# Graph network in four layers: TensorE adds half of the attention heads while turning them, elu in four VectorE operations, convolution tables packed side by side

## What is computed

```python
edge_index = jnp.stack([src, dst])
x = _layernorm(x + _L0_gnn_ref(x, edge_index, edge_weight, ...))   # two TAG convolutions of 5 hops
x = _layernorm(x + _L1_gnn_ref(x, edge_index, ...))                # mean aggregation, then attention with 4 heads
x = _layernorm(x + _L2_gnn_ref(x, edge_index, edge_weight1, ...))  # sum/mean convolution
x = _layernorm(x + _L3_gnn_ref(x, edge_index, ...))                # attention with 4 heads, dense layer
```

```python
def _tag_conv(x, row, col, norm, W, b):        # layer 0, called twice
    out = x @ W[0]
    h = x
    for k in range(1, K + 1):                  # K = 5
        h = jax.ops.segment_sum(h[row] * norm[:, None], col, num_segments=N_NODES)
        out = out + h @ W[k]
    return out + b
# end of layer 1: out is the mean of the heads
out = (out - mu) * jax.lax.rsqrt(var + 1e-05) * gamma + beta
return jax.nn.elu(out)
```

## Time and profile before

| | |
|---|---|
| median of three runs | 10347.91 us (10343.13 to 10349.23) |
| the profiled execution's own time | 10350.19 us |
| its span in the trace | 10348.5 us |
| PE, PEld, DVE busy | 56%, 28%, 57% of the span |
| ACT, POOL busy | 31%, 67% |
| granted TensorE clock, mean | 0.768 |
| DMA | 1016.84 MB, mean 98 GB/s |

### The profile page before, as it was taken

One profiled execution on the slowest core, in us unless ns is written; L12 is line 12 of the kernel. 1 busy time (PEld: TensorE's weight loads), 2 busy tenths in 40 slices (PEclk: granted clock), 3 DMA queues, 4 the chain that ended last, 5 costly groups with the idle time before them and its releaser, 6 DMA issues. The chain is left out here.

```text
span 10348.5 us, 86417 instructions
## 1 busy us (share of the span) xinstructions
PE 5760.6 (56%) x19261; PEld 2887.3 (28%) x19261; DVE 5897.1 (57%) x16861; ACT 3169.7 (31%) x5395; POOL 6886.8 (67%) x6659
## 2 busy tenths in 40 slices
PE   1672465555566984555555400598885776720277
PEld 0331232333333542222222200243222333410143
DVE  2341565556555656666666578544449994520697
ACT  0351233333332322222222201244443553310144
POOL 7777777777777747777777777775750006767477
PEclk9796677777777996676666655799998997755698
DMA  4620332222224752222222222222333442222353
GB/s 130 202 84 20 84 109 89 89 86 92 87 90 156 245 206 83 89 88 85 86 89 86 82 74 80 69 72 57 72 61 111 146 139 63 75 52 52 81 151 121
DMA packets 967572, 1016.84 MB, mean 98 GB/s; under 512 B 530229, under 2 KB 584231, under 8 KB 954507
## 3 DMA queue, kind: packets, MB, share of 16 engines
q1 hardware_dynamic: 754186, 880.78, 26.3%
q0 software_dynamic: 212864, 130.53, 7.1%
HBM read 491.86 MB, written 596.27 MB: 105 GB/s over the span
## 5 line engine op out<-in xcount | busy, mean ns | idle before, releaser
L710 POOL DMA_INDIRECT gathered<-u,place_of_source x1564 | 1645.0, 1052 | 522.5 <-issue 476.3
L710 POOL DMA_INDIRECT gathered<-hop,place_of_source x1564 | 1615.0, 1033 | 530.4 <-issue 492.0
L763 DVE SCALAR_TENSOR_TENSOR first_node_sum<-sums,ends_first,first_node_sum 128x64 f32<-128x64 f32 x4680 | 1302.7, 278 | 8.3 <-DVE sums L753 6.8
L739 DVE TENSOR_TENSOR weighted<-gathered,bank 128x512 f32<-128x512 f32 (+1 forms) x490 | 335.6, 685 | 1407.5 <-DMA gathered<-hop,place_of_source 625.3
L753 DVE SCALAR_TENSOR_TENSOR sums<-sums,same_as_before,weighted 128x64 f32<-128x64 f32 x3900 | 1079.3, 277 | 69.0 <-DVE weighted L739 41.9
L710 POOL DMA_INDIRECT gathered<-x,row_of_source x782 | 806.3, 1031 | 300.0 <-issue 224.0
L480 PE MATMUL bank<-dense_tmp,mean 128*128 128x512 f32 x980 | 569.5, 684 | 37.4 <-ACT dense_tmp L489 31.7
L2187 POOL DMA_INDIRECT out_dram<-lane_out,node_to_write x392 | 407.2, 1039 | 274.5 <-ACT lane_out L2108 160.2
L710 POOL DMA_INDIRECT gathered<-y,place_of_source x391 | 406.8, 1040 | 233.0 <-issue 118.9
L710 POOL DMA_INDIRECT first_sum<-head_sums,row_of_first_end x2 | 2.0, 1025 | 827.9 <-DMA head_sums<-head_sums 827.6
L710 POOL DMA_INDIRECT pair<-h_sage,row_of_source x391 | 404.6, 1035 | 220.5 <-issue 125.6
(11 more groups left out here) (446 smaller groups left out, 15158.6 us busy)
## 6 DMA issues: line engine op xcount, KB each, us to landing
head_sums<-head_sums SPq DMA_DIRECT2D x98, 1024.0 KB, 4.7
y<-conv_out SPq DMA_DIRECT2D x294, 256.0 KB
conv_out<-y SPq DMA_DIRECT2D x245, 256.0 KB, 3.3
hop<-sums SPq DMA_DIRECT2D x196, 256.0 KB, 2.1
turned<-rows_turned SPq DMA_DIRECT2D x196, 256.0 KB, 2.7
cat<-turned SPq DMA_DIRECT2D x196, 256.0 KB
u<-conv_out SPq DMA_DIRECT2D x196, 256.0 KB, 2.0
lane_raw<-x SPq DMA_DIRECT2D x196, 256.0 KB
```

Of the source, the lines that this page charges most:

```text
L710: return e.indirect_dma_start(out=into, out_offset=None, in_=tab, in_offset=bass.IndirectOffsetOnAxis(ap=index, axis=0), bounds_check=top, ...
L739: e.tensor_tensor(weighted[g % 2][:, 0:n, :], st.rows_of(g), over(st.weight[:, cols], D), ALU.mult).then_inc(st.weighed.handle, 1)
L763: e.scalar_tensor_tensor(h, row_, flast[:, t:t + 1], h, ALU.mult, ALU.add).then_inc(st.headed.handle, 1)
```

## The change

Three edits, and buffers to suit.

- `attend` of layer 1: VectorE adds `head_sums` to `heads` for the second pair of heads only, in one operation of 128x1024. For the first pair (c = 0) the four transposes become eight matmuls with the identity as moving operand, which turn `heads` and `head_sums` and add them in the bank. `head_sums` gets a fourth buffer, and a slot waits for the last turn of group g - 4 in place of `ended` of g - 3. `attend` of the last layer stays as it was.
- elu in four VectorE operations: gamma is the scalar of the first product; beta enters as the bias of ScalarE's exponential, as -beta in a maximum, and, centred, in the last norm. The chain of a lane is two steps shorter (31 steps in `attend`, 57 in the dense blocks). This holds for the dense blocks too.
- Stage `top`: tables 1 and 2, tables 3 and 4, and x and the fifth hop's sums lie side by side over 128 partitions, so `conv_mult` runs three times with contraction over 128 (six matmuls in place of twelve). x is loaded into `both` beside the sums, in pieces of 256 bytes. `hid` has four buffers; ScalarE adds the bias before it drains the products of g - 1; VectorE's order is sums of g, leaky relu of g - 1, odd products of g - 2.
- In the setup: one matmul and two small VectorE operations more, and six loads for `w0two` in place of two.

```diff
-    def norm_vector(e, W, r, n, o, y, centred=False, affine=False):
+    def norm_vector(e, W, r, n, o, y, centred=False, shift=None, scale=None):
         n += 4 if centred else 5
         yield W.n(r, n)
         for l in W.lanes(r):
             e.wait_ge(*W.at(r, l, n))
             c = W.b(y, l) if centred else W.bank[l][1][:, :]
-            e.tensor_tensor(W.b(o, l), c, W.b("tmp", l), ALU.mult).then_inc(W.chain[l].handle, 1)
-        if affine:
-            yield W.n(r, n + 1)
-            for l in W.lanes(r):
-                e.wait_ge(*W.at(r, l, n + 1))
-                e.tensor_scalar(W.b(o, l), W.b(o, l), wts["v_gamma"][:, 0:1], wts["v_beta"][:, 0:1],
-                                ALU.mult, ALU.add).then_inc(W.chain[l].handle, 1)
+            if shift is not None:
+                m = e.scalar_tensor_tensor(W.b(o, l), c, shift[:, 0:1], W.b("tmp", l), ALU.add, ALU.mult)
+            elif scale is not None:
+                m = e.scalar_tensor_tensor(W.b(o, l), c, scale[:, 0:1], W.b("tmp", l), ALU.mult, ALU.mult)
+            else:
+                m = e.tensor_tensor(W.b(o, l), c, W.b("tmp", l), ALU.mult)
+            m.then_inc(W.chain[l].handle, 1)
+    GAT_STEPS = 15
     def gat_scalar(e, W, r, n):
         yield from act(e, W, r, n, "a", None, ACT.Identity, b=1, v=wts["v_bg"])
         yield from norm_scalar(e, W, r, n + 1, "a", True)
-        yield from act(e, W, r, n + 8, "b", "b", ACT.Exp)
-        yield from norm_scalar(e, W, r, n + 11, "a")
+        yield from act(e, W, r, n + 6, "b", "a", ACT.Exp, v=wts["v_beta"])
+        yield from norm_scalar(e, W, r, n + 9, "a", shift=wts["v_cbeta"])
...
     def gat_vector(e, W, r, n, o, xT):
-        yield from norm_vector(e, W, r, n + 1, "a", "a", True, True)
-        yield W.n(r, n + 7)
-        for l in W.lanes(r):
-            e.wait_ge(*W.at(r, l, n + 7))
-            e.tensor_scalar(W.b("b", l), W.b("a", l), 0.0, None, ALU.min).then_inc(W.chain[l].handle, 1)
-        yield from stt(e, W, r, n + 9, "a", "a", 0.0, "b", ALU.max, ALU.add)
-        yield from stt(e, W, r, n + 10, "a", "a", -1.0, xT, ALU.add, ALU.add)
-        yield from norm_vector(e, W, r, n + 11, o, "a")
+        yield from norm_vector(e, W, r, n + 1, "a", "a", True, scale=wts["v_gamma"])
+        yield from stt(e, W, r, n + 7, "a", "a", wts["v_nbeta"][:, 0:1], xT, ALU.max, ALU.add)
+        yield from stt(e, W, r, n + 8, "a", "b", 1.0, "a", ALU.min, ALU.add)
+        yield from norm_vector(e, W, r, n + 9, o, "a", shift=wts["v_cbeta"])
...
-            cat = [sb(ctx, f"cat{i}", [P, HOPS, 512]) for i in range(2)]
+            both = [sb(ctx, f"x_and_sums{i}", [P, K8, 2, D]) for i in range(3)]
+            top_sums = [a[:, :, 1, :] for a in both]
...
+            cat = [sb(ctx, f"cat{i}", [P, 2, 2, 512]) for i in range(2)]
             turned_t = [sb(ctx, f"rows_turned{i}", [P, 512]) for i in range(4)]
-            hid = [sb(ctx, f"hidden{i}", [P, 512]) for i in range(2)]
+            hid = [sb(ctx, f"hidden{i}", [P, 512]) for i in range(4)]
             ybuf = [sb(ctx, f"conv_out{i}", [P, HOPS + 1, K8, D]) for i in range(2)]
...
-            def conv_turn(e, g, i):
-                n = 2 * g + i
-                if i:
+            def conv_turn(e, g, a):
+                if a == 0:
+                    e.wait_ge(*x_again[g % 3](16 * (g // 3 + 1)))
                     e.wait_ge(*top.ended(g))
-                else:
-                    e.wait_ge(*cat_in[g % 2](16 * HOPS * (g // 2 + 1)))
-                if n >= 2:
-                    e.wait_ge(*conv["moved"](n - 1))
-                two = sums[g % 3][:].rearrange("p k d -> p (k d)") if i else cat[g % 2][:, 0, :]
+                if g:
+                    e.wait_ge(*conv["moved"](2 * g + a - 1))
                 for q in range(4):
-                    t = e.transpose(PS[i][:, q * P:(q + 1) * P], two[:, q * P:(q + 1) * P], ident[:])
+                    t = e.transpose(PS[a][:, q * P:(q + 1) * P], both[g % 3][:, 2 * q + a, :, :].rearrange("p s d -> p (s d)"), ident[:])
                 t.then_inc(conv["turned"].handle, 1)
             def conv_mult(e, g, m):
-                k = (1, 2, 3, 4, 0, 5)[m]
-                if m == 0 and g:
-                    e.wait_ge(*conv["biased"](2 * g))
-                if k in (0, HOPS):
-                    n = 2 * g + k // HOPS
-                    e.wait_ge(*conv["moved"](n + 1))
-                    rhs = turned_t[n % 4][:, :]
-                else:
-                    rhs = cat[g % 2][:, k, :]
+                if m == 0:
+                    e.wait_ge(*cat_in[g % 2](16 * 4 * (g // 2 + 1)))
+                    if g:
+                        e.wait_ge(*conv["biased"](2 * g))
                 for a in range(2):
-                    half = slice(a * D, (a + 1) * D)
-                    t = e.matmul(PS[2 + a][:, :], wts["w0pair"][half, k, :], rhs[half, :], start=m == 0, stop=m == HOPS)
+                    n = 2 * g + a
+                    if m == 2:
+                        e.wait_ge(*conv["moved"](n + 1))
+                    rhs = turned_t[n % 4][:, :] if m == 2 else cat[g % 2][:, m, a, :]
+                    t = e.matmul(PS[2 + a][:, :], wts["w0two"][:, m, :], rhs, start=m == 0, stop=m == 2)
                 t.then_inc(conv["mult"].handle, 1)
...
             def conv_scalar(e, g):
                 conv_move(e, g, 0)
                 conv_move(e, g, 1)
+                e.wait_ge(*conv["mult"](3 * (g + 1)))
+                if g >= 2:
+                    e.wait_ge(*conv["product"](K8 * (g - 1)))
+                for a in range(2):
+                    e.activation(hid[2 * (g % 2) + a][:, :], PS[2 + a][:, :], ACT.Identity,
+                                 bias=wts["v_b0"][:, 0:1]).then_inc(conv["biased"].handle, 1)
                 if g:
                     conv_out_scalar(e, g - 1)
-                e.wait_ge(*conv["mult"](K6 * (g + 1)))
-                e.wait_ge(*conv["product"](K8 * g))
-                for a in range(2):
-                    e.activation(hid[a][:, :], PS[2 + a][:, :], ACT.Identity,
-                                 bias=wts["v_b0"][:, 0:1]).then_inc(conv["biased"].handle, 1)
             def conv_leak(e, g):
                 for a in range(2):
+                    h = hid[2 * (g % 2) + a][:, :]
                     e.wait_ge(*conv["biased"](2 * g + a + 1))
-                    e.scalar_tensor_tensor(hid[a][:, :], hid[a][:, :], 0.01, hid[a][:, :], ALU.mult,
-                                           ALU.max).then_inc(conv["hidden"].handle, 1)
+                    e.scalar_tensor_tensor(h, h, 0.01, h, ALU.mult, ALU.max).then_inc(conv["hidden"].handle, 1)
...
+                    tables = turned.rearrange("(m s g a f) c -> s g f m a c", m=2, s=2, g=NG, a=2)
                     def cat_load(g):
+                        if g >= 3:
+                            e.wait_ge(*conv["turned"](2 * (g - 2)))
+                        e.dma_start(both[g % 3][:, :, 0, :], columns(xc, g)).then_inc(x_again[g % 3].handle, 16)
                         if g >= 2:
-                            e.wait_ge(*conv["mult"](K6 * (g - 1)))
-                        e.dma_start(cat[g % 2][:, 0, :].rearrange("p (k d) -> p k d", d=D), columns(xc, g)
-                                    ).then_inc(cat_in[g % 2].handle, 16)
-                        for m in range(1, HOPS):
-                            e.dma_start(cat[g % 2][:, m, :], ttab[m - 1][g * P:(g + 1) * P, :]).then_inc(cat_in[g % 2].handle, 16)
+                            e.wait_ge(*conv["mult"](3 * (g - 1)))
+                        for m in range(2):
+                            for s in range(2):
+                                e.dma_start(cat[g % 2][s * D:(s + 1) * D, m, :, :], tables[s, g, :, m, :, :]).then_inc(cat_in[g % 2].handle, 16)
...
                         if g >= 3:
                             e.wait_ge(*conv["turned"](2 * (g - 2)))
-                        else:
-                            e.wait_ge(*rows_turned(HN))
-                            e.wait_ge(*hops[-1].stored[g](16 * in_slots(3, lambda g: 1)[g]))
-                        paced_sums(e, top, g, sums[g % 3], sums[(g - 1) % 3], none, 0, 0, False)
-                        if g >= 3:
-                            conv_out_vector(e, g - 3)
+                        paced_sums(e, top, g, top_sums[g % 3], top_sums[(g - 1) % 3], none, 0, 0, False)
+                        if g:
+                            conv_leak(e, g - 1)
                         if g >= 2:
-                            conv_leak(e, g - 2)
...
-        LAST = HD + (17 if v2 else 6)
+        LAST = HD + (GAT_STEPS if v2 else 6)
+        NS = 4 if v2 else LANES
...
+                        if v2 and c == 0:
+                            yield W.n(j, 2 + 3 * i)
+                            e.wait_ge(*W.at(j, 0, 2 + 3 * i))
+                            for n in range(4):
+                                lo = n * 2 * W4 + q * W4
+                                to = W.bank[0][0][:, n * P:(n + 1) * P]
```

(18 more changed lines are left out.)

70 lines of the change are left out of this document (37 added, 33 removed).

## The result

The kernel after takes 10211.11 us (median of four runs, 10208.99 to 10214.55), the kernel before 10348.56 beside it (median of four): ratio 0.9869, interval 0.9855 to 0.9884. The forecast was 10217, faster by more than 0.2%. The profiled execution took 10209.65 us, with a span of 10207.9.

A forecast was written before the change was run, and what follows sets the result against it. The limit changes by stage: gathers mostly, TensorE in `top`, VectorE in layer 1's `attend`. From 10350.2 us, less 88 (`attend`), 31 (`top`) and 12 (gathers), it reached 10219, or 10217 against the runs' median; range 10185 to 10290.

The forecast's parts named there:

- What bounds the kernel: Whole kernel: gathers set the pace, except in layer 1's `attend` and `top`, where GpSimd waits 827.6 and 114.2 us.
- Attend, VectorE's side: Layer 1's `attend`: the addition saves 1.20 us, elu 0.92, so VectorE's slot falls from 14.48 to 12.36 us.
- Attend, TensorE's side: Layer 1's `attend`: TensorE's slot becomes 12.0 us, VectorE still sets the slot, 12.6 us with 0.24 added; 88 us saved.
- The small matmuls: Layer 1's `attend`: sixteen float32 matmuls of 128 columns replace eight transposes, at 0.25 us each, between 0.22 and 0.41.
- rival (a): Layer 1's `attend`: TensorE holds the slot with 1.4 us of waits, slot 13.4, saving 51 us: 10254; chance 0.18.
- rival (e): Layer 1's `attend`: a granted clock of 0.74 makes the slot 16.2 us, 80 us lost: 10385; chance 0.05.
- Top: Stage `top`: the new order saves 0.49 us a group, 23 us, and the start 8, together 31 us.
- The DMA share: Stage `top`: loading x in 256-byte pieces costs nothing; the share rises from 0.73 to 0.93 at most.
- Gathers and dense blocks: Dense blocks: without two elu operations the gathers get shorter, 12 us in all, between 4 and 98.
- Rival (c): Dense blocks: the two removed operations blocked GpSimd for their whole time, 98 us in place of 12: 10131; chance 0.03.
- Rival (b): Stage `top` gives nothing, because VectorE drains the odd products too late and TensorE waits: 10248; chance 0.10.
- (d): Small matmuls cost 0.41 us, TensorE's slot in `attend` is 14.5 as before, `top` gives nothing: 10336; chance 0.04.

The follow-up runs named there:

- no_sums_turned: The kernel after, with the first pair of heads turned by four transposes without `head_sums`, which the result then lacks for these heads: 10246.2 us, ratio 0.9900.
- order_alone: The kernel before with only `top`'s new ScalarE and VectorE order and four hidden buffers; old tables and twelve matmuls: 12286.9 us, ratio 1.0016, on a slower chip.
- after_again: The kernel after, unchanged, run again on the first kind of chip: 10207.4 us, ratio 0.9863 to the kernel before.
- attend_both: The kernel before with elu in four operations and half of the additions on TensorE, stage `top` as before: 10261.5 us, ratio 0.9919.
- elu_alone: The kernel before with only elu in four VectorE operations, in `attend` and the dense blocks: 12255.7 us, ratio 0.9987, on a slower chip.
- heads_alone: The kernel before with only half of the additions on TensorE and the fourth `head_sums` buffer in layer 1's `attend`: 12239.2 us, ratio 0.9984, on a slower chip.

## Why the prediction was right, point by point

The time was right to 6 us. That is luck in part: by the first profile `attend` gave 12 us less than its term, `top` 15 more, and all the rest 19 in place of 12. The forecast was 131 us less; the two profiled executions differ by 140.5 and the medians by 137.4.

- *What bounds the kernel.* Right: the two waits of GpSimd gave 74.4 + 40.8 = 115 of the 140 us.
- *Attend, VectorE's side.* The addition: 1.20 forecast, 2.42 - 1.23 = 1.19 measured. The two operations of elu: right. The four that stay: I left them at 0.68; three of them read a scalar for each partition and take 0.06 more each, with 0.01 for the fourth 0.19 a slot, 9 us in all. VectorE's slot is 12.36 + 0.19 = 12.55, near the slot of 12.60 in `no_sums_turned`.
- *Attend, TensorE's side.* The small matmuls: 0.22 measured, 0.25 taken, 0.22 to 0.41 as bounds. The load is hidden, as the transposes suggested. The failed step is "VectorE still sets the slot, but only just". TensorE's queue sets it, so rival (a) describes the mechanism. Its price came out too high in the work and about right in the waits. By the prediction's own prices, with 0.22 for the small matmuls, TensorE's work is 6.2 + 1.8 + 16 x 0.22 = 11.5 us, not 12.0. The other 12.95 - 11.5 = 1.45 are what its order holds, where 1.4 was priced; of them the profile shows 0.57 as idle and the rest as busy. The forecast had put 0.24 on this, and on VectorE's slot. Slot 12.95 in place of 12.6; 75.6 us in place of 88.
- *The clock.* I used it only against the change, in rival (e). Its weight was on the other side: at a mean of 0.86 the elu edit alone gives nothing, without the turns of `head_sums` it is 0.91 and 39 us are lost, and the added matmuls are what keeps it at 1.00. The prediction took VectorE's savings to be additive. One at a time they are not (25 and 0 us); that they nearly were together is because TensorE was filled in the same change, which the prediction gave no credit for. This is luck too.
- *Top.* The mis-sized terms are the tables, the start and the end. The order did what was said, 0.53 us a group by `order_alone` where 0.49 was forecast: no wait for the bias, and products stalled by 0.16 a group (0.3 taken). `conv_mult` fell from 5.35 to 5.16, where I had put the packed tables at nothing: 0.19 x 48 = 9 us. Of the tables' 0.21 by `order_alone` the rest are the turns (0.97 there, 0.87 here), less 0.08 that the products take longer. That the two halves of a contraction over 64 do work side by side holds, since the saving is 4% and not half. The group: 11.45 in place of 11.7. The start: the products of group 0 wait until 3246.58, 6.8 us earlier, but 1.1 of these were gained before the stage, so 5.7 (8 taken). 48 x 0.74 + 5.7 = 41.2 us; the other 4.5 are at the end of the stage, where the kernel before has waits of 1.69 and 2.16 us before its last turns and products that the kernel after hasn't, and which I had put at nothing. Sum 45.7 in place of 31, inside the bounds of 0 to 47 (47.5 in the pair of `after_again` and `attend_both`).
- *The DMA share* of `top` was put at 0.93 at most and is 0.97: I had counted x's pieces, which are a quarter of the rise, and not what else the tables' loads bring.
- *Gathers and dense blocks.* 12 taken; the hops and the stretch from y to the pair gathers gave 1.1 + 15.7 in the first profile, in `after_again` they gave 3.9 + 6.7, and in `attend_both` all up to the pair gathers gave 8.5. A gather of a hop takes 1.026 us on average in place of 1.033. Rival (c), 98 us, is out.
- *Rival (b)* is out by the period of `top`, *(d)* by the 0.22 us, *(e)* by the clock of 1.00.

## What to carry to other kernels

Before counting a saving on one engine, look at the granted clock and at the idle time of TensorE in that stage: where other engines' results pass through TensorE, a shorter slot of VectorE can be taken back by a slower chain, and work moved to TensorE can be worth more than the time it frees. Where two engines' sums for a slot are 12.0 and 12.4 us, add to each what its fixed order holds in round trips (here some 1.4 us on TensorE, of which the profile shows 0.57 as idle) before saying which one sets the slot. A wait that shows on one engine isn't yet its limit: take it away or shorten the work before it, and see whether the slot moves.

## What was new about the hardware

- Removing 2.7 us of matmuls a slot made a kernel 39 us slower, and adding as much for nothing made `attend` 34 us faster. The mean granted clock was 0.86 (`elu_alone`) and 0.91 (`no_sums_turned`) with TensorE idle for 1.1 to 1.8 us at a time, and 1.00 with idle times of 0.24 and 0.33. What brings a fall isn't settled: the same idle times left the clock at 1.00 in one slot of three, and whether more transposes would have kept it up as the matmuls did was not tried.
- In `heads_alone` the clock is 1.00 too, and VectorE still waits 0.6 to 0.8 us a slot for the exponential (slots of 13.87 to 14.12, VectorE's own 13.3). Its chain has two steps more and so another order of the lanes; that this is the reason was not tried. So a full clock alone doesn't make a saving on VectorE count.
- An operation of VectorE on 128x512 float32 takes 0.69 us with an immediate and 0.75 with a scalar for each partition.
- Eight matmuls of 128 columns, float32, with the identity as moving operand, alternate two tiles at 0.22 us each; six of 512 columns with contraction over 128 take 5.16 us where twelve over 64, two side by side, take 5.35.
- Chips differ: on two of them the same program takes 17 and 18% longer (12127 and 12261 us), above all in the stages that gather, while `attend` takes the same; and there `top` as a whole doesn't get shorter by this change (743 to 756 us before, 752 to 808 after).
